# First projections: parts of q and k stored once in DRAM and repeated when a head reads them; splitting on ScalarE, GpSimd and VectorE

## What is computed

```python
q = split_heads(x @ Wq + bq)
k = split_heads(x @ Wk + bk)
v = split_heads(x @ Wv + bv)
scores = jnp.einsum('bhid,bhjd->bhij', q, k)
rel = jnp.einsum('bhid,pd->bhip', q, rel_key)
bias = jnp.take_along_axis(rel, rel_idx, axis=3)
logits = jnp.where(causal, (scores + bias) * scale, -jnp.inf)
attn = jax.nn.softmax(logits, axis=-1)
out = jnp.einsum('bhij,bhjd->bhid', attn, v)
```

## Time and profile before

| quantity | value |
|---|---|
| median of 3 executions | 4478.52 us (4476.37 to 4480.85) |
| the profiled execution | 4480.28 us |
| its span, first to last instruction | 4478.4 us |
| mean granted TensorE clock | 0.968 |
| PE, DVE, ACT, POOL busy | 93%, 83%, 80%, 52% |
| projections end, attention's first transfer | 104.34 us |
| attention's last band read | 921.11 us |
| first transfer behind the attention | 957.21 us |
| in the projections, one operation: ACT L319, DVE L303, POOL L124 | 0.60, 0.74, 1.14 us |

### The profile page before, as it was taken

The page is one execution under the profiler, slowest core; times in us unless marked ns, Lnnn a source line. Parts: engine busy times, 40 slices in busy tenths (PEclk is TensorE's granted clock), DMA queues, the critical chain, the costliest instruction groups (busy, mean ns, idle before and its releaser), DMA issues. The chain is left out here.

```text
span 4478.4 us, 137304 instructions
## 1 busy us (share of the span) xinstructions
PE 4185.3 (93%) x44000; PEld 2964.7 (66%) x44000; DVE 3697.2 (83%) x8420; ACT 3591.3 (80%) x6842; POOL 2342.0 (52%) x2840
## 2 busy tenths in 40 slices
PE   4899999966999999999999999999999999999994
PEld 2466666643777777777777777777777777777773
DVE  6688888876888888888888888888888888888884
ACT  1799998944888888888888888888888888888882
POOL 1000000016766666666766666666666666666661
PEclk7899999977999999999999999999999999999996
DMA  6777777722111111111111111111111111111111
GB/s 224 219 234 230 228 226 229 234 77 70 37 45 41 44 37 38 45 41 45 35 40 44 41 45 35 43 41 41 45 35 43 40 41 45 36 42 40 45 40 49
DMA packets 258776, 359.63 MB, mean 80 GB/s; under 512 B 44404, under 2 KB 216156, under 8 KB 257884
## 3 DMA queue, kind: packets, MB, share of 16 engines
q1 hardware_dynamic: 258140, 351.55, 26.0%
HBM read 151.19 MB, written 93.34 MB: 55 GB/s over the span
## 5 line engine op out<-in xcount | busy, mean ns | idle before, releaser
L1369 PE MATMUL la_ps<-la_Wqkv,la_xsT 128*128 (+1 forms) x2304 | 1195.1, 614 | 6.4 <-DVE la_rsk L1083 3.5
L1026 POOL TENSOR_TENSOR la_rt<-la_rt,la_rn 128x1024 f32<-128x1024 f32 x384 | 722.9, 1904 | 27.5
L1083 DVE TENSOR_TENSOR la_rsq<-la_ps,la_tab 128x1024 f32<-128x1024 f32 x384 | 469.3, 1222 | 104.5 <-ACT la_sq L1227 101.4
L1227 ACT ACTIVATE la_sq<-la_ps 128x512 f32<-128x512 f32 x768 | 454.5, 596 | 90.1 <-PE la_ps L1369 28.2
L1090 DVE TENSOR_REDUCE la_ssum<-la_sq 128x8 f32<-128x512 f32 x768 | 502.3, 673 | 24.0 <-issue 24.0
L1404 PEld LDWEIGHTS la_ps<-la_kT,la_qB 128*64 128x64 f32 x12288 | 391.3, 138 | 146.1 <-issue 145.8
L1369 PEld LDWEIGHTS la_ps<-la_Wqkv,la_xsT 128*128 128x128 f32 x2304 | 378.1, 191 | 150.4 <-issue 109.7
L1083 DVE TENSOR_TENSOR la_rsk<-la_ps,la_tab 128x1024 f32<-128x1024 f32 x384 | 465.1, 1211 | 4.7 <-ACT la_sq L1227 4.4
L1435 PEld LDWEIGHTS la_ps<-la_Wo,la_oT 128*128 128x128 f32 x3072 | 366.7, 192 | 131.1 <-issue 130.3
L1404 PE MATMUL la_ps<-la_kT,la_qB 128*64 128x64 f32 x12288 | 434.1, 224 | 0.0
L475 POOL COPY at_vh<-V 128x64 f32 (+1 forms) x64 | 15.2, 238 | 785.6 <-PE at_ps L674 784.8
(11 more groups left out here) (168 smaller groups left out, 10272.7 us busy)
## 6 DMA issues: line engine op xcount, KB each, us to landing
at_band<-skew_scratch SPq DMA_DIRECT2D x64, 1536.0 KB, 7.3
la_vs<-la_v SPq DMA_DIRECT2D x192, 384.0 KB, 3.5
skew_scratch<-at_R SPq DMA_DIRECT2D x64, 1024.0 KB, 6.7
la_vs<-la_v SPq DMA_DIRECT2D x192, 128.0 KB, 3.4
la_Wqkv<-in_wqkv SPq DMA_DIRECT2D x28, 384.0 KB, 3.3
kt_scratch<-pr_k SPq DMA_DIRECT2D x24, 384.0 KB, 3.2
qt_scratch<-pr_q SPq DMA_DIRECT2D x24, 384.0 KB, 4.1
at_qh<-qt_scratch SPq DMA_DIRECT2D x64, 144.0 KB
```

Source lines behind the costliest of these rows:

```text
L1026: e.tensor_tensor(heads(rt, w), heads(rt, w), wide(rn[:, w * H:(w + 1) * H], D), ALU.mult)\
L1083: e.tensor_tensor(dst.rearrange("p f (h d) -> p f h d", d=D), ps[:, c % 2, :].rearrange("p (h d) -> p h d", d=D).unsqueeze(1).to_broadcast ...
L1227: e.activation(sq[:, c % 2, :], ps[:, c % 2, :], ACT.Square).then_inc(sq_ev.sem, 1)
L1369: e.matmul(ps[:, c % 2, :], xsT[:, m * P:(m + 1) * P], Wqkv[:, ds(layer(n) % 2, 1), c * 512:(c + 1) * 512], start=True, stop=True)\
```

## The change

(In the diff, the hunk with the semaphores' declarations is left out: `q_out` and `k_out` become one per buffer, of 80 and 48 counts, and `q3_ev`, `k3_ev` start two steps ahead.) The scratch tensors keep each part once: `qt` holds parts 0, 1, 2, 0, 1 of q for each head and `kt` parts 0, 1, 2 of k. `heads_in` builds the nine combinations with a source that repeats: 3 times 24 rows, for q with a step of one part between repeats, for k with a step of 0. A step writes 3 + 5 transfers of 128 KB instead of 3 + 3 of 384 KB.

ScalarE now evicts q and k, each twice: once as f32 and once as bf16, which is part 0. The remaining three operations (subtract, make part 1, subtract into part 2) are done for q by GpSimd and for k by VectorE. qf, kf, q3 and k3 have two buffers. In VectorE's body the split of k (step t-2) now stands behind the eviction of V (step t-1).

```diff
@@ -168,8 +168,8 @@
 def build(nc, a, out):
-    qt_d = nc.dram_tensor("qt_scratch", [PARTS, PARTS, P, B * S], BF16).ap()
-    kt_d = nc.dram_tensor("kt_scratch", [PARTS, PARTS, P, B * S], BF16).ap()
+    qt_d = nc.dram_tensor("qt_scratch", [H_A, 2 * PARTS - 1, D_A, B * S], BF16).ap()
+    kt_d = nc.dram_tensor("kt_scratch", [H_A, PARTS, D_A, B * S], BF16).ap()
     rel_d = nc.dram_tensor("rel_scratch", [PARTS, D_A, REL], BF16).ap()
@@ -193,8 +193,9 @@
         xh, xhT = t.sb("xh", [P, G, E]), t.sb("xhT", [P, G * P])
-        qf, kf = t.sb("qf", [P, G * P]), t.sb("kf", [P, G * P])
-        q3, k3 = t.sb("q3", [P, PARTS, G * P], BF16), t.sb("k3", [P, PARTS, G * P], BF16)
+        qf, kf = t.sb("qf", [P, 2, G * P]), t.sb("kf", [P, 2, G * P])
+        q3, k3 = t.sb("q3", [P, 2, PARTS, G * P], BF16), t.sb("k3", [P, 2, PARTS, G * P], BF16)
+        unit = t.sb("unit", [P, 1])
         relT, relD, rel3 = t.sb("relT", [D_A, REL]), t.sb("relD", [D_A, REL]), t.sb("rel3", [D_A, PARTS, REL], BF16)
@@ -244,14 +245,16 @@
                     for p in range(PARTS):
-                        e.dma_start(kt_d[p, :, :, cols].rearrange("a p c -> p a c"), k3[:]).then_inc(k_out.sem, 16)
+                        e.dma_start(kt_d[:, p, :, cols], k3[:, m, p, :]).then_inc(k_out[m].sem, 16)
                     e.wait_ge(q3_ev.sem, q3_ev.v(i))
-                    for p in range(PARTS):
-                        e.dma_start(qt_d[:, p, :, cols].rearrange("a p c -> p a c"), q3[:]).then_inc(q_out.sem, 16)
+                    for p in range(2 * PARTS - 1):
+                        e.dma_start(qt_d[:, p, :, cols], q3[:, m, p % PARTS, :]).then_inc(q_out[m].sem, 16)
+            for mark in q_out + k_out:
+                mark.open(e)
             rounds(e, body, STEPS, 2, 2)
             e.wait_ge(s_sk, 16 * 2 * TB)
-            e.wait_ge(q_out.sem, q_out.v(STEPS - 1))
-            e.wait_ge(k_out.sem, k_out.v(STEPS - 1))
+            for mark in q_out + k_out:
+                e.wait_ge(mark.sem, mark.v(STEPS // 2 - 1))
             e.wait_ge(rel_out.sem, rel_out.v(0))
@@ -263,15 +266,27 @@
             ln.open(e)
-            def body(t):
+            e.memset(unit[:], 1.0).then_inc(s_f, 1)
+            e.wait_ge(s_f, 3)
+            q3_ev.open(e)
+            def body(t):
+                for i, m in t.back(2):
+                    x, parts = qf[:, m, :], q3[:, m]
+                    e.wait_ge(q_ev.sem, q_ev.v(i))
+                    e.tensor_tensor(x, x, parts[:, 0, :], ALU.subtract).then_inc(c_q.sem, 1)
+                    e.wait_ge(c_q.sem, c_q.v(i, 1))
+                    e.tensor_tensor(parts[:, 1, :], x, unit[:].to_broadcast([P, G * P]), ALU.mult).then_inc(c_q.sem, 1)
+                    e.wait_ge(c_q.sem, c_q.v(i, 2))
+                    e.tensor_tensor(parts[:, 2, :], x, parts[:, 1, :], ALU.subtract).then_inc(q3_ev.sem, 1)
                 for i, m in t.back(0):
                     ln.root(e, i)
-            rounds(e, body, STEPS, 2, 0)
+            rounds(e, body, STEPS, 2, 2)
         @block.vector
         def _(e):
-            for mark in (v_ev, k_ev, k_out, q_out, q3_ev):
+            for mark in (v_ev, k3_ev):
                 mark.open(e)
@@ -291,26 +306,26 @@
                     ln.take(e, tiles_of(i), i)
-                for i, m in t.back(2):
-                    e.wait_ge(k_ev.sem, k_ev.v(i))
-                    e.wait_ge(k_out.sem, k_out.v(i - 1))
-                    split(e, c_k, i, kf[:], k3).then_inc(k3_ev.sem, 1)
-                    e.wait_ge(q_ev.sem, q_ev.v(i))
-                    e.wait_ge(q_out.sem, q_out.v(i - 1))
-                    split(e, c_q, i, qf[:], q3).then_inc(q3_ev.sem, 1)
                 for i, m in t.back(1):
-                    e.wait_ge(k_mm.sem, k_mm.v(i))
-                    e.tensor_scalar(kf[:], ps[:, 2, :], bkr[:, 0:1], None, ALU.add).then_inc(k_ev.sem, 1)
                     e.wait_ge(v_mm.sem, v_mm.v(i))
                     e.tensor_tensor(V[:, ds(i * G, G), :], ps[:, 3, :].rearrange("p (g d) -> p g d", g=G),
                                     over(bv[:], G), ALU.add).then_inc(v_ev.sem, 1)
+                for i, m in t.back(2):
+                    x, parts = kf[:, m, :], k3[:, m]
+                    e.wait_ge(k_ev.sem, k_ev.v(i))
+                    e.tensor_tensor(x, x, parts[:, 0, :], ALU.subtract).then_inc(c_k.sem, 1)
+                    e.wait_ge(c_k.sem, c_k.v(i, 1))
+                    e.tensor_copy(parts[:, 1, :], x).then_inc(c_k.sem, 1)
+                    e.wait_ge(c_k.sem, c_k.v(i, 2))
+                    e.tensor_tensor(parts[:, 2, :], x, parts[:, 1, :], ALU.subtract).then_inc(k3_ev.sem, 1)
             rounds(e, body, STEPS, 2, 2)
         @block.scalar
         def _(e):
-            for mark in (xhT_done, q_ev):
+            for mark in (xhT_done, q_ev, k_ev):
                 mark.open(e)
             e.wait_ge(s_in, 16 * N_IN)
+            e.wait_ge(s_bk, 3)
@@ -318,8 +333,16 @@
                     e.wait_ge(q_mm.sem, q_mm.v(i))
-                    e.wait_ge(q3_ev.sem, q3_ev.v(i - 1))
-                    e.activation(qf[:], ps[:, 1, :], ACT.Identity, bias=bqs[:, 0:1], scale=-SC_A).then_inc(q_ev.sem, 1)
+                    e.wait_ge(q3_ev.sem, q3_ev.v(i - 2))
+                    e.wait_ge(q_out[m].sem, q_out[m].v(i // 2 - 1))
+                    e.activation(qf[:, m, :], ps[:, 1, :], ACT.Identity, bias=bqs[:, 0:1], scale=-SC_A)
+                    e.activation(q3[:, m, 0, :], ps[:, 1, :], ACT.Identity, bias=bqs[:, 0:1], scale=-SC_A)\
+                        .then_inc(q_ev.sem, 1)
+                    e.wait_ge(k_mm.sem, k_mm.v(i))
+                    e.wait_ge(k3_ev.sem, k3_ev.v(i - 2))
+                    e.wait_ge(k_out[m].sem, k_out[m].v(i // 2 - 1))
+                    e.activation(kf[:, m, :], ps[:, 2, :], ACT.Identity, bias=bkr[:, 0:1])
+                    e.activation(k3[:, m, 0, :], ps[:, 2, :], ACT.Identity, bias=bkr[:, 0:1]).then_inc(k_ev.sem, 1)
             rounds(e, body, STEPS, 2, 1)
@@ -437,9 +460,11 @@
                 hd = n % HEADS_A
-                row, col = ds(hd % H_A * D_A, D_A), ds(hd // H_A * S, S)
-                for dst, src in ((qh, qt_d), (kh, kt_d)):
-                    e.dma_start(dst[:, m, :], src.rearrange("a b p c -> (a b) p c")[:, row, col])\
+                col = hd // H_A * S
+                for dst, src, step in ((qh, qt_d, D_A * B * S), (kh, kt_d, 0)):
+                    head = src[ds(hd % H_A, 1), 0:PARTS, :, ds(col, S)].rearrange("h a d c -> (h a d) c")
+                    e.dma_start(dst[:, m, :], bass.AP(head.tensor, head.offset, [[step, PARTS]] + list(head.ap)))\
                         .then_inc(qk_in[m % 2].sem, 16)
```

More of the change, by code:

```diff
@@ L204, in first_projections @@
         q_ev, k_ev, v_ev = (t.mark(n, 1, 1) for n in ("qe", "ke", "ve"))
-        q3_ev, k3_ev, rel3_ev = t.mark("q3", 1, 1), t.mark("k3"), t.mark("r3")
-        q_out, k_out, rel_out = t.mark("qo", 16 * PARTS, 1), t.mark("ko", 16 * PARTS, 1), t.mark("ro", 16)
-        c_q, c_k, c_rel = (t.mark(n, 2 * PARTS - 2) for n in ("cq", "ck", "cr"))
+        q3_ev, k3_ev, rel3_ev = t.mark("q3", 1, 2), t.mark("k3", 1, 2), t.mark("r3")
+        q_out, k_out, rel_out = [t.mark(f"qo{u}", 80, 1) for u in range(2)], [t.mark(f"ko{u}", 48, 1) for u in range(2)], t.mark("ro", 16)
+        c_q, c_k, c_rel = t.mark("cq", 2), t.mark("ck", 2), t.mark("cr", 2 * PARTS - 2)
         block = t.block()
```

## The result

| | median | range, executions | ratio to before, 95% |
|---|---|---|---|
| before | 4478.24 us | 4476.37 to 4480.85, 4 | 1 |
| changed | 4722.89 us | 4720.52 to 4731.11, 4 | 1.0549 [1.0531, 1.0567] |

The change is 244.7 us slower; 97 were forecast, and the time lies above the range. Spans of the profiled executions: 4718.7 against 4478.4 us, +240.3. By place: the projections end at 128.38 instead of 104.34 us (+24.0), the attention takes 128.38 to 1200.18 = 1071.8 instead of 852.9 us (+218.9), the rest -2.7.

What follows compares the result with a forecast made beforehand. PE was taken to set a head's pace, with the DMA round 1.2 us behind and overtaking it after the change. Terms 3.5 + 2.3 + 97.7 - 6.2 = +97.3 us gave 4577.6 us; bounds 4499 to 4656, each side widened by 4.

Steps and rivals of the forecast that it cites:

- three engines: Attention's head loads: three DMA engines instead of nine carry them, 2.65 us more a head (3.9 at the slower rate).
- PE sets the pace of a head: Attention before the change: PE, busy 196.5 of 200 us, fixes a head at about 12.7 us.
- DMA round after: 11.6 + 2.65 = 14.25 us: Attention: band read, loads, write and landing take 14.25 us (13.0 to 15.5) and set the pace; 63 rounds, +97.7 us.
- 1.2 us of slack: Attention before: the DMA round closes after 11.6 us of a 12.78 us period, leaving about 1.2 us to cover longer loads.
- the rival of hidden loads: Attention: loads spread as before or, issued two heads ahead, hurt nobody; only projections count, 4484 us; chance 0.12.
- The clock falls: Attention: waits in every head lower PE's clock; about 4620 us with a fifth affected, some 4850 with half; chance 0.05.
- a clock under 1.00 in the attention: Attention: a granted clock under 1.00 there was listed as a sign that the prediction is wrong.
- +2.3: Start of the attention: the first pair of loads lands later, two times 2.0 us instead of 1.0 + 0.66.
- -6.2 us for slack used up once: Attention: a band read lands before its first use, so 6.2 us of lateness costs nothing, once.
- Projections: +3.5 us: Projections: seven turns of 10.2 us instead of 9.14, then the remaining writes; end at 107.8 instead of 104.34 us.
- The serial path: Projections: normalise, wait for V's product, evict V, split k run one after another, 10.2 us a turn instead of 9.14.
- All lie below the turn, so neither engine binds: Projections: ScalarE's added evictions (3.4 us a turn in all) and GpSimd's added 3.8 us fit within a turn.

Runs made afterwards that it cites:

- e4_pad: The change plus 47 one-column memsets on VectorE behind its projections, so its attention loop begins at 231 as before the change; 4699.49 us, ratio 1.0473.
- e5_twelve_pad: e4_pad with each load of a head issued as three transfers of 24 rows, same bytes read as often; 4514.17 us, ratio 1.0073.
- e6_mix_pad: e5_twelve_pad with only k's load split in three, q's left one transfer with its repeat of three; 4556.89 us, ratio 1.0165.
- e2_shift: The kernel before plus 81 one-column memsets on VectorE behind its projections, so its attention loop begins at 312; 4602.53 us, ratio 1.0259.
- e8_noq_pad: e4_pad without GpSimd's three operations on q (parts 1 and 2 are zeros), all transfers kept; 4682.93 us, one execution.
- e3_nine: The change with the nine combinations stored and read as in the kernel before; 4626.87 us, ratio 1.0314.

## Why the prediction was wrong

Profiled executions, by experiment: projections +24.0; three engines, as the attention of e4_pad less that of before, 1048.0 - 852.9 = +195.1; stalls of VectorE, 1071.8 - 1048.0 = +23.8; the rest -2.7. Sum +240.2.

- **What bounds the kernel before, and where.** Right in the place: all behind the attention kept its time, and the loads decided. "PE sets the pace of a head" is not borne out: the round is closed by the loads, as shown below.
- **Three engines.** Right: share 0.19, and e5_twelve_pad gives the cost back.
- **"DMA round after: 11.6 + 2.65 = 14.25 us".** The round itself came between its bounds of 13.0 and 15.5: in the change 4.9 us in most rounds from band read to write and 8.6 to its landing, 13.5 us. The step that failed is the next: that this round sets the pace, that 1.2 us of slack cover it, and that SP waits for the write. In e4_pad, from the fourth round on, the write has landed 1.0 to 2.8 us before each band read, and DVE's last minimum ends 0.12 us before it. The chain that closes last goes through PE: band read, loads issued, loads landed, PE's first product with them, DVE's minimum, next band read. The steps of this chain, means over the last 60 rounds in us, with the landings taken from the trace's semaphore events:

| run | band read to first load | to landing of both loads | to PE's first product with them | to next band read | round |
|---|---|---|---|---|---|
| before | 0.96 | 7.49 | 0.19 | 4.09 | 12.73 |
| e5_twelve_pad | 0.92 | 7.76 | 0.17 | 4.09 | 12.94 |
| e6_mix_pad | 0.93 | 8.39 | 0.21 | 4.10 | 13.63 |
| e4_pad | 0.90 | 9.48 | 0.54 | 4.84 | 15.77 |

Timeline of SP and PE, one round of before (it begins in the earlier trace rows, with the first load at 402.65) and, in a second fence, one of e4_pad:

```profile
410.15 0.28 PE L638 MATMUL at_ps<-at_relD,at_qh 72*128 72x256 bf16 x1
...
414.24 0.36 SPq L455 DMA_DIRECT2D at_band<-skew_scratch  x1
```

```profile
508.25 0.80 SPq L470 DMA_DIRECT2D at_qh<-qt_scratch  x1
...
523.53 0.36 SPq L483 DMA_DIRECT2D at_band<-skew_scratch  x1
```

Before, from first load to first product it is 7.50 us, and 4.09 more to the band read; in e4_pad it is 9.56 (the product starts at 517.81, shown above) and 5.72. In the kernel before PE's first product starts within 0.2 us of the landing in 50 of the 60 rounds, so the loads had no slack to lose. The earlier trace rows had said that they came just in time, with 0.7 us of waiting in all; the text used it for the rival of hidden loads. The loads are also not issued two heads ahead, as that rival says: PE uses them in the same round. The forecast had made the loads 2.65 us longer and let the slack take part of it, +1.55 us a head; they land 1.99 us later, and all of it counts, 125 us in 63 heads.
- **"The clock falls", a rival with 0.05.** It came beside the forecast instead of in its place, and makes the rest of e4_pad's round: 0.35 us more from landing to first product and 0.75 from there to the band read, 1.10 us a head or 69 us. The last step takes at most 4.1 us in 23 rounds of e4_pad and 4.65 to 5.73 us in the other 37, whose clock in that step is 0.61 to 0.70; in 15 rounds PE comes 1.5 to 1.9 us late to loads that have landed, after working at the lower clock. PE is busy 182.2 of 200 us, so 14.35 of 15.75 us a head, against 196.5 / 200 x 12.7 = 12.48 before; 12.48 / 0.86, the granted clock there, is 14.5. e6_mix_pad shows the landing's part without the clock's: loads 0.90 us later, round 0.90 us longer, 12.56 us of PE a head at 1.00. The argument against the rival went by the mean busy share of 0.87; e4_pad has 0.91 and still a clock of 0.86, and a clock under 1.00 in the attention was one of the prediction's own signs of being wrong. No run held the clock up under the full waits, so the split rests on these rows.
- **Start and end of the attention.** From its first transfer to the first band read e4_pad takes 3.0 us more than before, near the +2.3. The -6.2 us for slack used up once did not come: from the last band read to the next part it is 36.1 us in both kernels.
- **Code of VectorE: no term at all.** Removing instructions moved the loop behind them. Alone that costs 118 us (e2_shift), more than the whole forecast; here it costs 24. In the turn with the stalls the loads have landed 4.5 us or more before PE comes to them, so their lateness costs nothing there, and the three other heads of an iteration take (4 x 16.13 - 19.3) / 3 = 15.1 instead of 15.75 us.
- **"Projections: +3.5 us".** 24.0 came. The turn was to be 10.2 us and took (102.27 - 40.02) / 5 = 12.45, so seven times 2.25 = 15.8 us more. The serial path was right, since e8_noq_pad has 10.2; the failed step is "All lie below the turn, so neither engine binds": GpSimd's operations need not bind to stretch VectorE's. The tail took 12.6 instead of 8.3 us: its 16 transfers are issued without a gap, 0.64 us each, while the DMA engines are 0.74 busy from 117 to 127 us at 202 GB/s, so SP's issuing sets its length and not the 288 GB/s of the forecast. The about 1 us before the first byte is seen in the kernel before: of the band read issued at 414.24 us the first packet starts at 415.26. SP's timeline:

```profile
115.76 1.85 SPq L248 DMA_DIRECT2D kt_scratch<-pr_k  x3
117.66 3.18 SPq L251 DMA_DIRECT2D qt_scratch<-pr_q  x5
120.88 1.90 SPq L248 DMA_DIRECT2D kt_scratch<-pr_k  x3
122.83 3.18 SPq L251 DMA_DIRECT2D qt_scratch<-pr_q  x5
128.38 1.16 SPq L455 DMA_DIRECT2D at_relD<-rel_scratch  x3
```

## What to carry to other kernels

Before a load's source is given another outermost dimension, ask how many engines will then carry it, and how late it may land: if the first use starts right behind the landing, there is no slack, even where the wait list shows a few tenths of a microsecond. Follow the chain from that use to the next issue, and not only the transfers. Where PE gets a new wait in every turn, add a price for work at the lower clock; here it was 69 us beside 125 from the landing. And when a change adds or removes instructions ahead of a long loop, look for regular stalls with no releaser and for instruction packets in the DMA part, and undo the shift with padding before anything else is judged.

## What the runs showed of the hardware beyond that

**Instruction packets come during a stall.** Window 508 to 512 us of the change, DMA queues:

```profile
q1 hardware_dynamic: 1149, 1.41, 105.5%
q14 instruction: 2, 0.02, 2.0%
```

Two packets of 8 KB arrive while DVE stands still before 512.28, and two more from 512 to 517 us. From 500 to 560 us, within one iteration, there are 5. From 400 to 600 us the three runs with stalls have 15 (the change), 16 (e2_shift) and 19 (e3_nine), and the eleven without have none. The whole kernel has 356 to 367 such packets in those three and 277 to 297 in the eleven. That the packets are the loop's code and that VectorE waits for them is the author's reading, from the name of their queue and from when they come; the trace names nothing that ends the stall. Nor do the runs show why a loop that begins at 184 or 312 has them in every iteration and one at 231, 251 or 291 has not.

**The clock after a stall** (the change, columns as above):

```profile
500.00:510.00 10.00, 8.62 (x66) 6.19 (x64) 6.54 (x26) 8.54 (x16) 0.24 (x1) 1.00 0.58 190
510.00:513.00 3.00, 0.00 (x0) 0.00 (x0) 0.72 (x2) 0.00 (x0) 0.00 (x0) 0.59 0.88 275
513.00:517.00 4.00, 3.97 (x17) 1.84 (x17) 1.91 (x8) 1.83 (x3) 0.00 (x0) 0.50 0.18 56
517.00:522.00 5.00, 5.00 (x41) 3.19 (x37) 4.08 (x13) 3.86 (x7) 0.24 (x1) 0.96 0.00 0
```

PE idles these 3 us, and its following 4 us of work go at a granted clock of 0.50. The records of the granted clock hold two shares only, 1.00 and 0.50. In the kernel before, the next product starts 0.215 to 0.227 us after one of 512 columns in bf16 (L648) at 1.00, and five of six times 0.400 to 0.427 us after it at 0.50. That is 2.3 to 2.4 columns a ns at the one share and 1.2 to 1.3 at the other, and all that the trace has of the 2.4 and 1.2 GHz of the text ahead. e2_shift shows both parts of a stall's cost: PE waits 66.1 / 11 = 6.0 us an iteration for DVE's copy, and at its clock of 0.92 (178.09 us busy in 400 to 600 us) works 178.09 / 200 x 14.6 = 13.0 us a head instead of 12.48, 2.1 us more an iteration of four; together 8.1, against 118 / 15 = 7.9 measured.

**GpSimd beside VectorE.** VectorE's three operations of 128x512 on k take 1.08, 0.80 and 1.21 us on average beside GpSimd's (the change) and 0.68, 0.43 and 0.69 without (e8_noq_pad).
